# Linear attention: rotary pairs 64 partitions apart, halves exchanged by ScalarE, sine product and sum on GpSimd

## Chip, cores and metric

The kernel runs on one core of a Trainium2 chip. The metric is the device time of one execution in microseconds (us). TensorE is called PE, VectorE DVE, ScalarE ACT, GpSimd POOL and SyncE SP, as in the profile. SP issues all DMA transfers that this text speaks of.

## The reference

Sixteen sequences of 512 tokens with 128 features go through two layers. The stage that is changed here is the first one, causal linear attention with 16 heads of 8 features. Queries and keys are rotated by position, mapped by elu + 1, and the output at each token is a sum over all earlier tokens:

```
x = x + y                                  # y: depthwise convolution of 3 taps, then w_pw
qkv = einsum('btd,ed->bte', x, w_qkv)
q, k = _apply_rope(q, sin, cos), _apply_rope(k, sin, cos)
    # r1 = x1*cos - x2*sin ; r2 = x1*sin + x2*cos, pairs of neighbouring features
q_phi, k_phi = elu(q) + 1, elu(k) + 1
num   = q_phi . cumsum(k_phi * v)          # per head
denom = sum(q_phi * cumsum(k_phi))
attn  = num / (denom + 1e-6)
x = x + sigmoid(delta @ w_gate + b_gate) * (attn @ w_o)   # delta: x minus the token before
```

After it come a mixture of four experts, a routed layer, softmax attention and a second routed layer. They are left as they are.

## The kernel before

The stage is `attention_front`. It works on one sequence at a time, with features on the partitions and the 512 tokens along the free dimension. It is a software pipeline, written out by hand: each engine has a function `steps(b, u, n, f, c_)` that runs its share of one step, and `stages` calls it 19 times (the middle twelve in a loop of six rounds of two). In step s the engines work on four sequences at once: n = s is normalised, convolved and projected; f = s - 1 gets its rotary embedding and its feature map (q and k phi); b = s - 2 gets scores, state and weighted sum; c_ = s - 3 is divided, gated and normalised again. In a step with all four parts each engine goes through its list in the order written, and stops at the first wait that is not met. What other engines do does not change that order.

The names that matter here:

- `X` holds the input. SP loads sequence n with one transfer of 256 KB (L303). `stats(n)` on DVE (L700 and L703) is the first thing of a step on DVE and waits for that transfer; all of DVE's step stands behind it.
- `project` (L402) multiplies by the weights of q (n = 0) and k (n = 1) on PE. Each has two products, one with plain weights into bank 1 or 3 of PSUM (L409) and one with the weights of the exchanged pairs into bank 2 or 4 (L410).
- `rotate` (L706) on DVE multiplies bank 1 or 3 by the cosine and bank 2 or 4 by the signed sine, into `rot`. `rotated` (L714) adds the two and 1. `exps` (L614) on ACT makes the exponential `ex`, `phi` (L720) on DVE takes min(ex, 1) and the maximum with rot, into `qphi` or `kphi`.
- `stack` (L305) on SP copies qphi and kphi within SBUF into `qr` and `kr`, so that each head's 8 features lie on 8 neighbouring partitions at 0, 32, 64 or 96. It issues 4 transfers of 64 KB for q and 4 for k, each with 32 partitions as source and 8 as destination. `COPIES` is what their semaphores count to in a step.
- `scores` (L427) on PE multiplies kr by qr, 16 small products for each of 4 tiles t into banks 1 to 4. For t = 0 it waits until the projections of the next sequence have been read out of these banks (`qk_read`), and for the copies. `mask_scores` (L744) on DVE masks three of the banks into `am`, `raw_scores` (L618) on ACT copies the fourth, and `mask_last` (L341) on POOL masks it.
- `update_state` (L448) on PE and `mask_state` (L734) on DVE carry the sum over earlier tokens.
- `divide` (L756) on DVE is the division for c_; it waits for `copy_rdT` (L638) on ACT, and that for `turn_spread` (L487) on PE at the end of a step. `gate_tanh` (L643) is the gate on ACT.

In SP's list a step is: load X of n, then the copies for f. The load for step s therefore stands behind the copies that are issued in step s - 1.

Of the kernel before, what the change touches and what calls it, by code (L numbers as in the profile page):

```python
# [56 lines left out]
def _columns():  # L57
    at = 0
    for name, n in [("pw", P), ("q", P), ("qs", P), ("k", P), ("ks", P), ("v", P), ("o", P), ("gate", P),
                    ("moe_gate", MOE), ("dw", 3), ("b_gate", 1), ("ln_g", 1), ("ln_b", 1),  # L60
                    ("b1", MOE * MOE_CHUNKS), ("b2", MOE), ("router0", EXPERTS),
                    ("q1", P), ("k1", P), ("v1", P), ("router1", EXPERTS), ("br1", EXPERTS),
                    ("gamma", P), ("beta", P)]:
        WCOLS[name] = (at, at + n)
        at += n
    return at
# [122 lines left out]
def attention_front(nc, sems, X, w, c, PS, before, ones, minus_half, eps, scratch, H, LG, x):  # L189
# [4 lines left out]
    with ExitStack() as ctx:  # L194
# [52 lines left out]
        delta_ready = sem("delta_ready")  # L247
        qk_psum = sem("qk_psum"); qk_read = sem("qk_read"); rot_step = sem("rot_step"); exp_ready = sem("exp_ready")
        phi_ready = sem("phi_ready"); v_psum = sem("v_psum"); v_ready = sem("v_ready")
# [15 lines left out]

        COPIES = 16 * 4

# [29 lines left out]
        @block.sync  # L297
        def _(sp):
            def load(b):

                after_previous(sp, x_in, b, 16)
                src = x[bass.ds(b, 1), :, :].rearrange("o (c p) d -> p (o c) d", p=P)
                sp.dma_start(X[:, bass.ds(b * CT, CT), :], src).then_inc(x_in, 16)  # L303

            def stack(b, u):  # L305


                for which, (src, dst, signal) in enumerate([(qphi, qr, q_stacked), (kphi, kr, k_stacked)]):
                    sp.wait_ge(phi_ready, 2 * b + which + 1)
                    for j in range(4):  # L310
                        sp.dma_start(dst[32 * j:32 * j + HD, u, :, :], src[32 * j:32 * j + 32, u, :]).then_inc(signal, 16)

            def steps(b, u, n, f, c_):
                if n is not None:
                    load(n)
                if f is not None:
                    stack(f, 1 - u)
            stages(sp, steps)
            sp.wait_ge(x_in, 16 * BATCHES)

        @block.gpsimd
        def _(pool):
# [31 lines left out]
            def differences(f, u, c_):  # L354
                pool.wait_ge(x1_ready, f + 1)
                if c_ is not None:
                    pool.wait_ge(gate_psum, c_ + 1)
                nc.gpsimd.tensor_tensor(delta[:, 1 - u, 1:], x1T[:, 1 - u, 1:], x1T[:, 1 - u, 0:SEQ - 1],
                                        ALU.subtract).then_inc(delta_ready, 1)

            def weigh_keys(f, u):
                pool.wait_ge(kp_ready, f + 1)
                after_previous(pool, den_psum, f)
                nc.gpsimd.tensor_tensor(prod[:, :], qphi[:, 1 - u, :], kp[:, :], ALU.mult).then_inc(prod_ready, 1)

            def steps(b, u, n, f, c_):
                if n is not None:
                    inverse_deviation(n, ln1_stats, mv, ve, ve1_done, rstd, rstd1_ready, shift, shift1_ready, xn_ready, negated)
                if f is not None:
                    differences(f, u, c_)  # L370
                if b is not None:
                    mask_last(b, 0)
                    keep_x1(b, u)
                    mask_last(b, 1)
# [11 lines left out]
        def _(pe):  # L386
# [15 lines left out]
            def project(b, u, name, n):  # L402
                pe.wait_ge(x1_ready, b + 1)
                after_previous(pe, qk_read, b, 2)
                if since(b, 2):
                    pe.wait_ge(am_ready, 12 * (b + (-1)) - (1 - n))
                    if n:
                        pe.wait_ge(raw_ready, 4 * (b + (-1)))
                nc.tensor.matmul(PS[:, 1 + 2 * n, :], w(name), x1T[:, u, :], start=True, stop=True)  # L409
                nc.tensor.matmul(PS[:, 2 + 2 * n, :], w(name + "s"), x1T[:, u, :],  # L410
                                 start=True, stop=True).then_inc(qk_psum, 1)

# [155 lines left out]
        def _(act):  # L568
# [45 lines left out]
            def exps(b, n):  # L614
                act.wait_ge(rot_step, 6 * b + 3 * n + 3)
                nc.scalar.activation(ex[:, n, :], rot[:, n, 0, :], ACT.Exp, bias=minus_one[:, 0:1]).then_inc(exp_ready, 1)

# [39 lines left out]

            def steps(b, u, n, f, c_):
                if b is not None:
                    copy_k(b)  # L660
                if c_ is not None:
                    gate_tanh(c_)
                if f is not None:
                    exps(f, 0)
                    exps(f, 1)
                if b is not None:
# [5 lines left out]
                if b is not None:  # L672
                    raw_scores(b, 1)
                if n is not None:
                    copy_xnT(n)
# [17 lines left out]
        def _(dve):  # L693
# [12 lines left out]
            def rotate(b, n):  # L706


                after_previous(dve, phi_ready, b, 2)
                dve.wait_ge(qk_psum, 2 * b + n + 1)  # L710
                nc.vector.tensor_tensor(rot[:, n, 0, :], PS[:, 1 + 2 * n, :], c("cos"), ALU.mult).then_inc(rot_step, 1)
                nc.vector.tensor_tensor(rot[:, n, 1, :], PS[:, 2 + 2 * n, :], c("sin"), ALU.mult).then_inc(qk_read, 1)

            def rotated(b, n):  # L714
                dve.wait_ge(rot_step, 6 * b + 3 * n + 1)
                dve.wait_ge(qk_read, 2 * b + n + 1)
                nc.vector.scalar_tensor_tensor(rot[:, n, 0, :], rot[:, n, 0, :], 1.0, rot[:, n, 1, :],
                                               ALU.add, ALU.add).then_inc(rot_step, 2)

            def phi(b, u, n, dst):  # L720
                dve.wait_ge(exp_ready, 2 * b + n + 1)
                after_previous(dve, (q_stacked, k_stacked)[n], b, COPIES)
                nc.vector.scalar_tensor_tensor(dst[:, u, :], ex[:, n, :], 1.0, rot[:, n, 0, :], ALU.min,
                                               ALU.max).then_inc(phi_ready, 1)

# [64 lines left out]
            def steps(b, u, n, f, c_):  # L790
# [6 lines left out]
                if f is not None:  # L797
                    rotated(f, 0)
                    rotate(f, 1)
                    rotated(f, 1)  # L800
                    phi(f, 1 - u, 0, qphi)
                if b is not None:
                    mask_scores(b, 0)
                    mask_state(b, 0)
                if f is not None:
                    phi(f, 1 - u, 1, kphi)
                if c_ is not None:
                    close(c_)
                if b is not None:
                    invert(b)  # L810
                    mask_scores(b, 1)
                    mask_state(b, 1)
                if c_ is not None:
                    stats2(c_)
# [1264 lines left out]
def _stacked_rows():  # L2079

    p = np.arange(P)
    return 32 * (p % 4) + HD * (p // 32) + p % 32 // 4

# [26 lines left out]
def _layout(i):  # L2110
# [4 lines left out]
    t = {  # L2115
        "pw": i["L0_attn_w_pw"].T, "q": qkv[:P][nat].T, "qs": qkv[:P][nat ^ 1].T, "k": qkv[P:2 * P][nat].T,
        "ks": qkv[P:2 * P][nat ^ 1].T, "v": qkv[2 * P:].T, "o": i["L0_attn_w_o"].T, "gate": i["L0_attn_w_gate"].T,
        "moe_gate": i["L0_attn_w_moe_gate"].T, "dw": i["L0_attn_w_dw"], "b_gate": col(i["L0_attn_b_gate"]),
# [35 lines left out]
```

## Time and profile before

| | us |
|---|---|
| median of 3 runs | 1526.29 |
| range of the 3 runs | 1525.73 to 1536.03 |
| profiled execution, its own time | 1526.64 |
| profiled execution, span | 1524.8 |
| busy: PE / DVE / ACT / POOL | 1296.3 / 1003.6 / 801.9 / 689.2 |

The span is the time from the first to the last instruction in the profile; 1.8 us of the execution's own time lie around it. The stage in question covers roughly the first 472 us of the span, so the busy figures of the whole say little about it. The rows below are read from the trace by stretch and by instruction. In a timeline row the first number is the start in us from the start of the span, the second the time from the start of the first to the end of the last instruction of the row; "x3" is how many there are, and the brackets say how long the engine had been idle before and what released it. SPq rows are DMA issues. In a row for a stretch, DMA share is the mean busy share of the 16 DMA engines, and PEclk 1.00 stands for 2.4 GHz and 0.50 for 1.2 GHz.

### The profile page before, as it was taken

What the parts mean: (1) busy time and instruction counts of PE and PEld (TensorE: products, weight loads), DVE (VectorE), ACT (ScalarE), POOL (GpSimd) and SP (SyncE); (2) the same over time, 40 slices, a digit from 0 to 9 for tenths busy, and PEclk for the clock granted to TensorE, in tenths of its full rate; (3) what the DMA queues carried; (4) which work ended last, traced back from release to release, by engine and by line L of the source; (5) the groups of instructions that cost most, each with busy time, mean ns of one, the idle gap of its engine ahead of it and who ended that gap; (6) DMA issues with size and microseconds to landing.
All of it is one profiled execution on the core that took longest, in us unless ns stands there. A gap on an engine that the chain in (4) does not pass through costs nothing. (4 is left out here: it accounts for less than half of the span.)

```text
span 1524.8 us, 34022 instructions
## 1 busy us (share of the span) xinstructions
PE 1296.3 (85%) x10546; PEld 1013.7 (66%) x10546; DVE 1003.6 (66%) x3454; ACT 801.9 (53%) x1647; POOL 689.2 (45%) x845
## 2 busy tenths in 40 slices
PE   3899999999983999999999992667399999749996
PEld 1566666666652888888888881556277776539996
DVE  3677878787844788888888884456467777512221
ACT  2344444444423766666666660455266666525553
POOL 2344444444420044353444535223557788426665
PEclk9999999999975999999999996899699999969998
DMA  2231313131103000000000001556401112169881
GB/s 76 35 42 23 41 21 41 21 41 21 28 2 83 1 8 16 7 14 7 7 14 7 14 8 43 148 168 179 137 25 56 56 58 61 43 230 314 261 259 35
DMA packets 61579, 101.02 MB, mean 66 GB/s; under 512 B 9698, under 2 KB 36331, under 8 KB 61120
## 3 DMA queue, kind: packets, MB, share of 16 engines
q1 hardware_dynamic: 51648, 78.58, 20.1%
q0 software_dynamic: 9856, 21.52, 4.6%
q8 instruction: 37, 0.61, 0.2%
q14 instruction: 38, 0.31, 0.1%
HBM read 62.96 MB, written 29.75 MB: 61 GB/s over the span
## 5 line engine op out<-in xcount | busy, mean ns | idle before, releaser
L1138 DVE TENSOR_TENSOR m_Sl<-m_S,m_Sh 128x512 fp32r<-128x512 f32 x256 | 175.0, 693 | 32.5 <-ACT m_S L1050 27.6
L1050 ACT ACTIVATE m_S<-PS,W 128x512 f32<-128x512 f32 x256 | 175.3, 685 | 33.6 <-PE PS L958 30.5
L1413 POOL DMA_INDIRECT rows<-r_row,r_posi x128 | 139.7, 1091 | 37.4 <-issue 37.3
L1399 POOL TENSOR_TENSOR r_soft<-r_euler,r_soft 128x32 f32<-128x32 f32 x16 | 86.8, 5427 | 133.0 <-DVE r_soft L1295 133.0
L1045 ACT ACTIVATE m_Sh<-PS,W 128x512 fp32r<-128x512 f32 x128 | 88.1, 689 | 105.9 <-PE PS L958 105.6
L751 DVE TENSOR_TENSOR am<-PS,C 128x512 f32<-128x512 f32 x192 | 119.4, 676 | 20.5 <-PE PS L443 20.5
L956 PE MATMUL PS<-m_HH,m_w1h 128*128 128x512 f32 x256 | 110.8, 433 | 14.2 <-DVE m_HL L1102 14.0
L1631 PEld LDWEIGHTS PS<-f_wt,f_hid 128*128 128x128 f32 x960 | 119.6, 192 | 4.0
L1631 PE MATMUL PS<-f_wt,f_hid 128*128 128x128 f32 x960 | 120.0, 276 | 0.0
L1620 PE MATMUL PS<-f_xT,f_wt 128*128 128x256 f32 x480 | 119.6, 387 | 0.0
L344 POOL TENSOR_TENSOR am<-am,C 128x512 f32<-128x512 f32 x64 | 81.3, 1271 | 78.1 <-ACT am L624 78.1
L968 PE MATMUL PS<-m_Sh,m_w2h 128*128 128x512 f32 x256 | 102.0, 398 | 0.0
L958 PE MATMUL PS<-m_HH,m_w1l 128*128 128x512 f32 x256 | 101.8, 398 | 0.0
L957 PE MATMUL PS<-m_HL,m_w1h 128*128 128x512 f32 x256 | 101.7, 397 | 0.0
L971 PE MATMUL PS<-m_Sl,m_w2h 128*128 128x512 f32 x256 | 101.0, 395 | 0.0
L969 PE MATMUL PS<-m_Sh,m_w2l 128*128 128x512 f32 x256 | 100.6, 393 | 0.0
L1612 PE MATMUL PS<-C,f_row 128*128 128x128 f32 x160 | 34.0, 296 | 72.0 <-DMA f_row<-rows 72.0
L1709 DVE TENSOR_TENSOR f_res<-PS,f_xb 128x256 f32<-128x256 f32 x40 | 17.0, 425 | 118.8 <-PE PS L1631 118.8
L1620 PEld LDWEIGHTS PS<-f_xT,f_wt 128*128 128x128 f32 x480 | 87.2, 195 | 8.7
L1663 ACT ACTIVATE f_hid<-PS,f_wt 128x256 f32<-128x256 f32 x160 | 62.7, 474 | 55.0 <-PE PS L1620 54.8
L1593 POOL DMA_INDIRECT out<-f_res,f_token x80 | 79.2, 990 | 26.2 <-issue 26.2
L471 PE MATMUL PS<-am,vm 128*32 128x128 f32 x2048 | 80.3, 285 | 8.5 <-DVE am L751 7.1
(245 smaller groups left out, 3222.1 us busy)
## 6 DMA issues: line engine op xcount, KB each, us to landing
f_wt<-wr SPq DMA_DIRECT2D x40, 578.0 KB, 4.6
f_row<-rows SPq DMA_DIRECT2D x40, 260.0 KB, 2.9
f_wt<-wr SPq DMA_DIRECT2D x40, 256.0 KB, 2.9
f_row<-rows SPq DMA_DIRECT2D x40, 132.0 KB, 2.1
mid<-f_res SPq DMA_DIRECT2D x40, 128.0 KB, 2.7
rows<-r_padding SPq DMA_DIRECT2D x16, 260.0 KB, 3.3
X<-x SPq DMA_DIRECT2D x16, 256.0 KB, 5.4
qr<-qphi SPq DMA_DIRECT2D x64, 64.0 KB
```

What stands on the lines that cost most here:

```text
L751: nc.vector.tensor_tensor(am[:, j, :].rearrange("p (g q) -> p g q", g=4), PS[:, 1 + j, :].rearrange("p (g q) -> p g q", g=4), c("tri").uns ...
L956: nc.tensor.matmul(bank, w1h[:, f], HH[:, v, :], start=True, stop=False)
L957: nc.tensor.matmul(bank, w1h[:, f], HL[:, v, :], start=False, stop=False)
L958: nc.tensor.matmul(bank, w1l[:, f], HH[:, v, :], start=False, stop=True).then_inc(h_psum, 1)
L968: nc.tensor.matmul(bank, w2h[:, f], Sh[:, n % 4, :], start=(k == 0), stop=False)
L969: nc.tensor.matmul(bank, w2l[:, f], Sh[:, n % 4, :], start=False, stop=False)
L971: last = nc.tensor.matmul(bank, w2h[:, f], Sl[:, n % 4, :], start=False, stop=(k == MOE_CHUNKS - 1))
L1050: nc.scalar.activation(S[:, n % 3, :], PS[:, n % 3, :], ACT.Silu, bias=w("b1")[:, n:n + 1]).then_inc(s_ready, 1)
L1138: nc.vector.tensor_tensor(Sl[:, n % 4, :], S[:, n % 3, :], Sh[:, n % 4, :].bitcast(F32), ALU.subtract).then_inc(sl_ready, 1)
L1413: nc.gpsimd.indirect_dma_start(out=self.rows, out_offset=bass.IndirectOffsetOnAxis(ap=self.posi[:, u, t:t + 1], axis=0), in_=self.row[:, u ...
L1620: mm = nc.tensor.matmul(PS[:, 2 + 2 * (u % 2) + bank, half * SLOT:(half + 1) * SLOT], wt[:, u, f * P:(f + 1) * P], xT[:, u % 2, :], start= ...
L1631: mm = nc.tensor.matmul(PS[:, 6 + v, a * P:(a + 1) * P], hid[:, v, f, a * P:(a + 1) * P], wt[:, u, (chunks + f) * P:(chunks + f + 1) * P], ...
```

## The change

The features are laid out in another order over the partitions, so that the two features of a rotary pair lie 64 partitions apart. The projections with exchanged weights are gone. ACT copies partitions 64 to 127 of the projection to 0 to 63 and 0 to 63 to 64 to 127 (`swap_halves`), POOL multiplies this copy by the sine and adds it to DVE's product with the cosine (`sum_rotated`). elu + 1 is now min(exp, 1) + relu, with the relu on ACT. k needs one bank of PSUM instead of two, and its phi moves on DVE to a later place. With the new order of features one head's 8 features come from two halves, so each copy into qr or kr is split in two, of 16 partitions to 4.

```diff
-        COPIES = 16 * 4
+        COPIES = 16 * 8
                     for j in range(4):
-                        sp.dma_start(dst[32 * j:32 * j + HD, u, :, :], src[32 * j:32 * j + 32, u, :]).then_inc(signal, 16)
+                        for o in range(2):
+                            to = 32 * j + HD // 2 * o
+                            sp.dma_start(dst[to:to + HD // 2, u, :, :],
+                                         src[64 * o + 16 * j:64 * o + 16 * j + 16, u, :]).then_inc(signal, 16)
...
+            def sum_rotated(f, n):
+                pool.wait_ge(qk_read, 2 * f + n + 1)
+                nc.gpsimd.tensor_tensor(rot[:, n, 1, :], rot[:, n, 1, :], c("sin"), ALU.mult).then_inc(sin_done, 1)
+                pool.wait_ge(sin_done, 2 * f + n + 1)
+                nc.gpsimd.tensor_tensor(rot[:, n, 0, :], rot[:, n, 0, :], rot[:, n, 1, :], ALU.add).then_inc(rot_summed, 1)
...
                 if f is not None:
+                    sum_rotated(f, 0)
                     differences(f, u, c_)
                 if b is not None:
                     mask_last(b, 0)
+                if f is not None:
+                    sum_rotated(f, 1)
+                if b is not None:
                     keep_x1(b, u)
...
-                    pe.wait_ge(am_ready, 12 * (b + (-1)) - (1 - n))
-                    if n:
-                        pe.wait_ge(raw_ready, 4 * (b + (-1)))
-                nc.tensor.matmul(PS[:, 1 + 2 * n, :], w(name), x1T[:, u, :], start=True, stop=True)
-                nc.tensor.matmul(PS[:, 2 + 2 * n, :], w(name + "s"), x1T[:, u, :],
-                                 start=True, stop=True).then_inc(qk_psum, 1)
+                    pe.wait_ge(am_ready, 12 * (b + (-1)) - (2 - n))
+                nc.tensor.matmul(PS[:, 1 + n, :], w(name), x1T[:, u, :], start=True, stop=True).then_inc(qk_psum, 1)
...
             def exps(b, n):
-                act.wait_ge(rot_step, 6 * b + 3 * n + 3)
-                nc.scalar.activation(ex[:, n, :], rot[:, n, 0, :], ACT.Exp, bias=minus_one[:, 0:1]).then_inc(exp_ready, 1)
+                act.wait_ge(rot_summed, 2 * b + n + 1)
+                nc.scalar.activation(ex[:, n, :], rot[:, n, 0, :], ACT.Exp)
+                nc.scalar.activation(rot[:, n, 1, :], rot[:, n, 0, :], ACT.Relu).then_inc(exp_ready, 1)
+
+            def swap_halves(b, n):
+                act.wait_ge(cos_done, 2 * b + n + 1)
+                for o in range(2):
+                    ins = nc.scalar.activation(rot[64 - 64 * o:128 - 64 * o, n, 1, :], PS[64 * o:64 * o + 64, 1 + n, :], ACT.Copy)
+                ins.then_inc(qk_read, 1)
...
             def steps(b, u, n, f, c_):
+                if f is not None:
+                    swap_halves(f, 0)
                 if b is not None:
                     copy_k(b)
                 if c_ is not None:
                     gate_tanh(c_)
                 if f is not None:
+                    swap_halves(f, 1)
                     exps(f, 0)
-                    exps(f, 1)
...
                     raw_scores(b, 1)
+                if f is not None:
+                    exps(f, 1)
...
-                nc.vector.tensor_tensor(rot[:, n, 0, :], PS[:, 1 + 2 * n, :], c("cos"), ALU.mult).then_inc(rot_step, 1)
-                nc.vector.tensor_tensor(rot[:, n, 1, :], PS[:, 2 + 2 * n, :], c("sin"), ALU.mult).then_inc(qk_read, 1)
-
-            def rotated(b, n):
-                dve.wait_ge(rot_step, 6 * b + 3 * n + 1)
-                dve.wait_ge(qk_read, 2 * b + n + 1)
-                nc.vector.scalar_tensor_tensor(rot[:, n, 0, :], rot[:, n, 0, :], 1.0, rot[:, n, 1, :],
-                                               ALU.add, ALU.add).then_inc(rot_step, 2)
+                nc.vector.tensor_tensor(rot[:, n, 0, :], PS[:, 1 + n, :], c("cos"), ALU.mult).then_inc(cos_done, 1)
...
-                nc.vector.scalar_tensor_tensor(dst[:, u, :], ex[:, n, :], 1.0, rot[:, n, 0, :], ALU.min,
-                                               ALU.max).then_inc(phi_ready, 1)
+                nc.vector.scalar_tensor_tensor(dst[:, u, :], ex[:, n, :], 1.0, rot[:, n, 1, :], ALU.min,
+                                               ALU.add).then_inc(phi_ready, 1)
...
                 if f is not None:
-                    rotated(f, 0)
                     rotate(f, 1)
-                    rotated(f, 1)
-                    phi(f, 1 - u, 0, qphi)
                 if b is not None:
                     mask_scores(b, 0)
                     mask_state(b, 0)
                 if f is not None:
-                    phi(f, 1 - u, 1, kphi)
+                    phi(f, 1 - u, 0, qphi)
                 if c_ is not None:
                     close(c_)
                 if b is not None:
                     invert(b)
                     mask_scores(b, 1)
                     mask_state(b, 1)
+                if f is not None:
+                    phi(f, 1 - u, 1, kphi)
```

SP's list changes in the copies. One step of it in the program before, ahead of the loop (a row is line, operation, destination, source, shape of the destination, count; X is the input, qr and kr the stacked copies):

```order
L303 DMA X<-x 128x4x128
L311 DMA qr<-qphi 8x4x512 x4
L311 DMA kr<-kphi 8x4x512 x4
L303 DMA X<-x 128x4x128
L311 DMA qr<-qphi 8x4x512 x4
```

And the same place now:

```order
L303 DMA X<-x 128x4x128
L313 DMA qr<-qphi 4x4x512 x8
L313 DMA kr<-kphi 4x4x512 x8
L303 DMA X<-x 128x4x128
L313 DMA qr<-qphi 4x4x512 x8
```

Between two loads of X there are now 16 transfers instead of 8, each to 4 partitions instead of 8.

DVE's list for one step with all four parts, from the statistics' aggregation on, before (L711 and L712 are the products with cosine and sine, L717 the sum, L723 phi, L751 the masks of the scores, L736 that of the state, L759 the division):

```order
L711 TENSOR_TENSOR rot<-PS,C 128x512
L712 TENSOR_TENSOR rot<-PS,C 128x512
L759 TENSOR_TENSOR attn<-PS,spread 128x512
L717 SCALAR_TENSOR_TENSOR rot<-rot 128x512
L711 TENSOR_TENSOR rot<-PS,C 128x512
L712 TENSOR_TENSOR rot<-PS,C 128x512
L717 SCALAR_TENSOR_TENSOR rot<-rot 128x512
L723 SCALAR_TENSOR_TENSOR qphi<-ex,rot 128x512
L751 TENSOR_TENSOR am<-PS,C 128x512 x3
L736 TENSOR_TENSOR state<-PS,C 128x128
L723 SCALAR_TENSOR_TENSOR kphi<-ex,rot 128x512
```

And now (L731 is the product with the cosine, L736 phi, L749 the state's mask, L764 the masks of the scores, L772 the division, L777 and L780 `close`, L753 and L755 `invert`):

```order
L731 TENSOR_TENSOR rot<-PS,C 128x512
L772 TENSOR_TENSOR attn<-PS,spread 128x512
L731 TENSOR_TENSOR rot<-PS,C 128x512
L764 TENSOR_TENSOR am<-PS,C 128x512 x3
L749 TENSOR_TENSOR state<-PS,C 128x128
L736 SCALAR_TENSOR_TENSOR qphi<-ex,rot 128x512
L777 SCALAR_TENSOR_TENSOR x2T<-th,PS 128x512
L780 TENSOR_TENSOR x2T<-x2T,x1c 128x512
L753 TENSOR_SCALAR den<-PS 128x64
L755 RECIPROCAL den<-den 128x64
L764 TENSOR_TENSOR am<-PS,C 128x512 x3
L749 TENSOR_TENSOR state<-PS,C 128x128
```

The row that follows is phi of k. Two products and both sums are gone from DVE, phi of q stands behind the first masks, and phi of k behind the second ones.

## Rows read from the trace of the kernel before

**Rows 1.** Stretches, six rounds: length, busy time per engine, clock, DMA share, GB/s.

```profile
core 0: us, PE busy (x) PEld busy (x) DVE busy (x) ACT busy (x) POOL busy (x), PEclk, DMA share, GB/s
200.00:354.00 154.00, 143.67 (x1976) 100.05 (x1974) 121.60 (x290) 76.10 (x169) 66.76 (x96) 1.00 0.24 31
```

**Rows 2.** Timeline of DVE, statistics that open a step: start, us, what, idle before.

```profile
43.44 0.88 DVE L700 BATCH_NORM_STATS2 st<-X 128x6 f32<-128x128 f32 x4 [9.65 <-DMA X<-x]
...
65.81 0.86 DVE L700 BATCH_NORM_STATS2 st<-X 128x6 f32<-128x128 f32 x4
...
270.26 0.86 DVE L700 BATCH_NORM_STATS2 st<-X 128x6 f32 x4
...
372.92 0.86 DVE L700 BATCH_NORM_STATS2 st<-X 128x6 f32 x4
```

**Rows 3.** Timeline of one round, all engines: start, us, what, idle before.

```profile
251.34 0.68 DVE L712 TENSOR_TENSOR rot<-PS,C 128x512 f32<-128x512 f32 x1
...
252.27 1.17 PE L443 MATMUL PS<-qr,kr 8*128 8x128 f32 x32 [0.49 <-DVE rot L712]
...
253.37 0.68 DVE L723 SCALAR_TENSOR_TENSOR qphi<-ex,rot 128x512 f32<-128x512 f32 x1
...
255.76 0.27 DVE L736 TENSOR_TENSOR state<-PS,C 128x128 f32<-128x128 f32 x1
...
255.96 0.67 DVE L723 SCALAR_TENSOR_TENSOR kphi<-ex,rot 128x512 f32<-128x512 f32 x1
...
257.04 2.82 SPq L311 DMA_DIRECT2D kr<-kphi  x4
...
259.49 1.82 DVE L751 TENSOR_TENSOR am<-PS,C 128x512 f32<-128x512 f32 x3
...
260.18 0.39 SPq L303 DMA_DIRECT2D X<-x  x1
...
265.92 0.60 ACT L593 ACTIVATE x1T<-PS 128x512 f32<-128x512 f32 x1 [2.07 <-PE PS L399]
...
267.72 1.27 POOL L364 TENSOR_TENSOR prod<-qphi,kp 128x512 f32<-128x512 f32 x1 [1.91 <-DVE kp L731]
...
269.80 1.12 PE L409 MATMUL PS<-x1T,W 128*128 128x512 f32 x2 [0.78 <-DVE am L751]
...
271.82 0.69 DVE L711 TENSOR_TENSOR rot<-PS,C 128x512 f32<-128x512 f32 x1 [0.28 <-PE PS L410]
...
275.23 0.69 DVE L759 TENSOR_TENSOR attn<-PS,spread 128x512 f32<-128x512 f32 x1 [2.12 <-ACT spread L640]
```

**Rows 4.** Lines L303 and L311: issue time in ns, min/median/max; landing of X.

```profile
L303 SPq DMA_DIRECT2D X<-x x16: 385/398/443, 8.8 to 362.8; - x16
...
DMA to landing us min/median/max: 2.8/5.4/5.8
...
L311 SPq DMA_DIRECT2D kr<-kphi x64: 659/672/1184, 34.8 to 413.5; - x64
```

**Rows 5.** Stretches while only the copies of qphi and kphi move (columns as rows 1).

```profile
257.00:261.00 4.00, 3.75 (x64) 3.09 (x56) 3.13 (x7) 2.07 (x6) 1.98 (x3) 1.00 0.56 63
...
258.40:259.40 1.00, 1.00 (x11) 1.00 (x11) 0.61 (x2) 0.23 (x2) 1.00 (x2) 1.00 0.52 51
```

**Rows 6.** Stretches around the idle time of PE in step 1 (columns as rows 1).

```profile
30.00:33.00 3.00, 0.00 (x0) 0.00 (x0) 2.64 (x5) 1.92 (x5) 0.00 (x0) 1.00 0.00 0
33.00:36.00 3.00, 1.08 (x4) 0.71 (x4) 0.79 (x1) 1.73 (x7) 1.26 (x1) 0.57 0.39 84
...
39.00:42.00 3.00, 2.31 (x5) 0.85 (x4) 0.00 (x0) 0.60 (x1) 0.00 (x0) 0.79 0.91 88
```

**Rows 7.** Timeline of step 1: first DVE product, qphi, PE after its idle time.

```profile
26.90 0.69 DVE L711 TENSOR_TENSOR rot<-PS,C 128x512 f32<-128x512 f32 x1 [9.61 <-PE PS L410]
...
30.97 0.68 DVE L723 SCALAR_TENSOR_TENSOR qphi<-ex,rot 128x512 f32<-128x512 f32 x1
...
34.62 1.08 PE L393 MATMUL PS<-C,xn 128*128 128x128 f32 x4 [5.14 <-ACT vm L611]
```

More of the change, by code:

```diff
@@ L58, in _columns @@
     at = 0
-    for name, n in [("pw", P), ("q", P), ("qs", P), ("k", P), ("ks", P), ("v", P), ("o", P), ("gate", P),
+    for name, n in [("pw", P), ("q", P), ("k", P), ("v", P), ("o", P), ("gate", P),
                     ("moe_gate", MOE), ("dw", 3), ("b_gate", 1), ("ln_g", 1), ("ln_b", 1),
@@ L247, in attention_front @@
         delta_ready = sem("delta_ready")
-        qk_psum = sem("qk_psum"); qk_read = sem("qk_read"); rot_step = sem("rot_step"); exp_ready = sem("exp_ready")
+        qk_psum = sem("qk_psum"); qk_read = sem("qk_read"); rot_summed = sem("rot_summed"); cos_done = sem("cos_done"); sin_done = sem("sin_done"); exp_ready = sem("exp_ready")
         phi_ready = sem("phi_ready"); v_psum = sem("v_psum"); v_ready = sem("v_ready")
@@ L2081, in _stacked_rows @@
     p = np.arange(P)
-    return 32 * (p % 4) + HD * (p // 32) + p % 32 // 4
+    return 32 * (p % 4) + HD * (p % 64 // 16) + 2 * (p % 16 // 4) + p // 64
 def _constants():
@@ L2115, in _layout @@
     t = {
-        "pw": i["L0_attn_w_pw"].T, "q": qkv[:P][nat].T, "qs": qkv[:P][nat ^ 1].T, "k": qkv[P:2 * P][nat].T,
-        "ks": qkv[P:2 * P][nat ^ 1].T, "v": qkv[2 * P:].T, "o": i["L0_attn_w_o"].T, "gate": i["L0_attn_w_gate"].T,
+        "pw": i["L0_attn_w_pw"].T, "q": qkv[:P][nat].T, "k": qkv[P:2 * P][nat].T, "v": qkv[2 * P:].T, "o": i["L0_attn_w_o"].T, "gate": i["L0_attn_w_gate"].T,
         "moe_gate": i["L0_attn_w_moe_gate"].T, "dw": i["L0_attn_w_dw"], "b_gate": col(i["L0_attn_b_gate"]),
```

## Prediction

> **What bounds the kernel now.** I first read the stretch of six rounds (a round is one pass through the step with all four parts) in the middle of the stage: of 154.0 us PE is busy 143.67, DVE 121.60, ACT 76.10, POOL 66.76 [rows 1]. So PE is nearly full, with DVE close behind. A round lasts (372.92 - 65.81) / 12 = 25.6 us, from the statistics that open step 3 to those that open step 15 [rows 2]. Taking work off PE and DVE could therefore pay, as long as nothing else becomes late. ACT and POOL have room.
>
> Next I read one round in order of time [rows 3], and asked of each wait what ends it last. PE waits for DVE's last read of the projections before it starts the scores (0.49 us), and for a DVE mask before the projection of q (0.78 us). DVE waits 2.12 us for the division's input at the turn of a step. The chain runs PE, ACT, DVE and back, with small waits everywhere.
>
> Third, SP. It shows no wait of an engine inside the loop, but it has a chain of its own: phi of q ends on DVE at 253.37 + 0.68 = 254.05, four copies of q, phi of k ends at 256.63, four copies of k from 257.04 on, and only then, at 260.18, the load of X [rows 3]. With a median of 5.4 us to its landing [rows 4] X is there at 265.6. The statistics need it at 270.26 [rows 2]. The slack is 4.7 us. Only in step 2 did DVE wait for X, 9.65 us [rows 2].
>
> **The change, what it takes away.** PE loses two products per round. One product takes 1.12 us from start to end [rows 3], less behind another one; I take 0.9, so 1.8 us of PE's 23.9 busy (143.67 / 6). The wait for the mask goes down by one mask, 0.6 us. DVE loses two products and two sums of 0.6 to 0.7 us, some 2.6 us.
>
> **What it adds on the chain.** Between DVE's product with the cosine and the scores now stand two ACT copies of 64 partitions. The nearest row is a copy of 128 x 512 out of PSUM, 0.60 us [rows 3]; one issued behind the other ends 0.5 later, so 1.1 us for a pair. Were time to go with partitions it would be 0.6; I keep 1.1, since nothing in the rows makes a narrower copy faster. POOL gets four operations of 1.27 us [rows 3] per round, 5.1 us, on an engine busy 11.1 of 25.6. ACT gets 2.2 us of copies and two relus of about 0.6. For q, POOL's pair, exp and relu take about 4 us behind the exchange and lie beside the scores and the state update; without that cover they would cost up to 2.
>
> **What it does to SP's chain.** There are two effects. First, phi of k moves behind the second masks: these end at 261.31, the state mask at about 261.5, phi at 262.2 instead of 256.63, 5.5 us later [rows 3]. Second, 16 transfers stand ahead of X instead of 8. SP's issue of one takes 0.67 us at 64 KB, while that of X takes 0.40 at 256 KB [rows 4], so bytes do not set it; 8 copies of k take 8 x 0.71 = 5.7 us to issue (2.82 / 4 each [rows 3]), half if it went with size.
>
> The service is dearer. While only these copies move, 9 of the 16 DMA engines are busy (0.56) and 63 GB/s flow [rows 5]: one transfer of 65.5 KB per 1.04 us. X, 4 times as large and spread over 128 partitions, lands in 2.8 us at best [rows 4]. So a transfer to 8 partitions is limited by where it goes. The new one goes to 4 partitions, each of which still gets 8 KB. I take the same 1.04 us for it, as if half the lanes did the same work each; the bound below is 0.52, half the bytes at the same rate, and the bound above 1.28, from the slowest stretch of 1 us, at 51 GB/s [rows 5].
>
> The Trainium skill ("DMA: Bandwidth & Descriptors", section "Why a DMA increments its semaphore by 16 and not by 1") says that a transfer runs on the largest number of engines up to 16 that divides the outermost dimension of both sides: 8 for 8 and 32 partitions, 4 for 4 and 16. The busy share agrees for the former; no row here shows the latter. The skill ("SBUF — State Buffer", section "Door 1: The DMA port swizzle") also has 4 neighbouring partitions share one port of 27.2 GB/s, an estimate of 54 GB/s for 8 partitions against the 63 measured, and 1.2 us for one new transfer. By it the sum would be 16 x 0.16 x 14 = 36 us more, 1655.
>
> **The new round.** Start with X landed, S.
> - Statistics until S + 1.3 (270.26 to where DVE began to wait, 271.82 - 0.28 [rows 2, 3]), then three DVE operations 0.61 apart: cosine of q, division, cosine of k, to S + 3.2.
> - ACT: q's exchange from S + 2.0 to 3.1, its copy of k and the tanh (0.6 each, as the copy's row) to 4.3, k's exchange to 5.4. Scores start at S + 5.5.
> - From the start of the scores to the state's mask it is 255.76 - 252.27 = 3.5 us [rows 3]; with mask (0.27) and phi (0.68), phi of q ends at S + 9.9.
> - From there to the landing of X it was 265.6 - 254.05 = 11.5 us with 8 transfers. Eight more at 1.04 make 19.8. The later phi of k hides in this: it ends about 6 us after phi of q, when q's eight are still being served (8.3 us).
>
> That closes a ring of 9.9 + 19.8 = 29.7 us, longer than 25.6: DVE waits for X in every step, and all that PE and DVE saved is idle time.
>
> **The clock.** PE then works 23.9 - 1.8 = 22.1 of 29.7 us, and most of the 7.6 idle is one piece ahead of the scores. In step 1 PE stood idle 5.14 us until 34.62 [rows 7]; the granted clock fell to 0.50 and stayed there until about 40.3 [rows 6], 5.6 us after work came back, at 1.2 instead of 2.4 GHz. That cost 2.8 us of work. The new round has 3.3 us of PE work between the start of the scores and the state update, on the ring. I charge 2.2 us, between 0 and 2.8 and near the row, since part may meet waits for DVE. The round is 31.9.
>
> **The sum.** Step 2: first cosine at 26.90 [rows 7], 0.9 earlier with one pair fewer; 0.7 product, 1.1 exchange, 2.6 POOL, 1.2 exp and relu, 0.7 phi, gaps 0.1 each: phi of q ends at 32.5 instead of 31.65 [rows 7]. With 43.44 - 31.65 = 11.8 and 8.3 more, statistics start at 52.6, +9.2. Step 2 to 3, without division, tanh and output projection: 19.8 + 7.6 + 2.2 = 29.6 against 22.37, +7.2. Twelve rounds at 31.9 - 25.6 = 6.3: +75.7. Behind step 15 no X is loaded; there I take nothing (PE gains 2, the clock takes it back). Together +92, on the profiled execution's own time of 1526.64, which is within 0.4 us of the median: 1619.
>
> **Rivals.**
> - *The clock holds.* PE's idle time falls into pieces. Then 13 x 2.2 = 29 us less: 1590. For it: the clock is 1.00 through all six rounds [rows 1], but there no idle piece is long. Chance 0.22.
> - *Copies served as fast as they are issued* (0.52 us each, below the 0.71 of the issue). Then only phi of k and the issue count: 262.2 + 0.4 + 5.7 + 0.3 = 268.6, landing 271.4 to 274.0, 1.1 to 3.7 late, of which the 2.12 us of DVE's idle time [rows 3] absorb most: 0 to 1.6 per round. The exchange takes back on the way to the scores what PE's products gave. With 4 to 6 us in step 2: 1531 to 1554, say 1543. For it: X's own rate. Chance 0.25, nearly half of it within 1%.
> - *Faster.* PE's relief decides. X would have to land within 8 us of the new phi of k (270.26 - 262.2), and the exchange stay hidden; then a round is 1.8 us shorter, 12 rounds 22 us: 1505. Against it: X landed 9.0 us after phi of k with half the transfers. Chance 0.05.
>
> **Numbers.** Main case 0.45, the clock holding 0.22, fast copies 0.25, faster 0.05, and 0.03 for worse than all. Range 1540 to 1655: from the middle of the fast-copy case up to two thirds of what transfers of 1.28 us would add (16 x 0.24 x 14 = 54 us); about 0.15 lies below and 0.05 above. A change under 1% can't be told from none. Faster by over 1% 0.05, within 1% 0.12, slower 0.83. The likeliest case's own range is 1600 to 1655.
>
> **What would show it.** In the profile after: statistics on DVE released by the DMA of X in 14 steps, for 5 us or more; a round of 32 us; a busy share near 0.27 while the copies move, with 30 GB/s; low clock in each round. If DVE waits for X only in step 2, the ring is wrong. If it waits and the share stays at 0.56, the service price is. If rounds last 29.7 with the clock at 1.00, only the clock is.

## The result and the profile after

The change makes the kernel slower: 1558.12 us (median of 4 runs, 1556.75 to 1558.82) against 1527.01 us, a ratio of 1.0203 with a 95% interval of 1.0181 to 1.0224. That is 31 us, where the prediction had 92. (A fourth run has moved the median of the kernel before from 1526.29 to 1527.01.) The profiled execution has a span of 1556.3 us, 31.5 more than before.

The page of the changed kernel gives the busy time of each engine, share of the span and instructions:

```profile
PE 1302.2 (84%) x10482; PEld 1022.8 (66%) x10482; DVE 970.5 (62%) x3390; ACT 853.4 (55%) x1743; POOL 775.1 (50%) x909
```

DVE works 33 us less than before, ACT 52 and POOL 86 us more. PE is at 1302.2 against 1296.3, although it has 64 matmul records fewer.

Where the time went is read as in [rows 2], from the statistics that open each step on DVE (start, duration, idle time before and its releaser):

```profile
47.73 0.87 DVE L720 BATCH_NORM_STATS2 st<-X 128x6 f32<-128x128 f32 x4 [9.50 <-DMA X<-x]
...
75.51 0.67 DVE L720 BATCH_NORM_STATS2 st<-X 128x6 f32<-128x128 f32 x3
```

```profile
266.12 0.87 DVE L720 BATCH_NORM_STATS2 st<-X 128x6 f32 x4 [1.12 <-DMA X<-x]
...
293.19 0.87 DVE L720 BATCH_NORM_STATS2 st<-X 128x6 f32 x4 [0.92 <-DMA X<-x]
```

```profile
402.38 0.87 DVE L720 BATCH_NORM_STATS2 st<-X 128x6 f32 x4 [1.04 <-DMA X<-x]
```

Step 2 opens at 47.73 instead of 43.44 (+4.3), step 3 at 75.51 instead of 65.81 (5.4 more), and the twelve rounds from step 3 to step 15 take 326.87 instead of 307.11, 27.24 us each instead of 25.59 (19.8 more). That makes 29.5 of the 31.5 us. The rest is scattered behind step 15. DVE waits for X in 13 steps (14 were forecast), but for 1 us in a round and not for 5 or more.

One round in order of time, all engines, to be read against [rows 3]:

```profile
268.87 0.69 DVE L772 TENSOR_TENSOR attn<-PS,spread 128x512 f32<-128x512 f32 x1 [0.88 <-ACT spread L656]
...
271.17 1.19 ACT L631 ACTIVATE rot<-PS 64x512 f32<-64x512 f32 x2
...
272.60 1.17 PE L452 MATMUL PS<-qr,kr 8*128 8x128 f32 x32 [2.35 <-ACT rot L631]
...
273.71 1.37 PE L512 MATMUL PS<-attn,W 128*128 128x512 f32 x2
273.76 1.89 DVE L764 TENSOR_TENSOR am<-PS,C 128x512 f32<-128x512 f32 x3 [3.61 <-PE PS L452]
...
274.87 1.91 PE L424 MATMUL PS<-W,x1T 128*128 128x128 f32 x8
...
277.14 1.14 PEld L480 LDWEIGHTS PS<-am,vm 128*32 128x32 f32 x32 [0.23 <-issue]
...
277.46 1.55 DVE L736 SCALAR_TENSOR_TENSOR qphi<-ex,rot 128x512 f32<-128x512 f32 x1
278.48 0.98 PEld L452 LDWEIGHTS PS<-qr,kr 8*128 8x128 f32 x32 [0.20 <-issue]
...
283.35 0.68 DVE L736 SCALAR_TENSOR_TENSOR kphi<-ex,rot 128x512 f32<-128x512 f32 x1
```

```profile
284.63 5.31 SPq L313 DMA_DIRECT2D kr<-kphi  x8
290.27 0.39 SPq L303 DMA_DIRECT2D X<-x  x1
```

The order of events is the one of the prediction. The exchange of k (L631, two copies, 1.19 us) ends at 272.36 and lets the scores start at 272.60, for which PE had waited 2.35 us; before it was 0.49 [rows 3]. The copies of k take 5.31 us to issue, and X is issued at 290.27, 2.9 us ahead of the statistics that need it. But X lands in 2.8 us, not in 5.4 and not behind a queue. Behind X there is a second wait that the prediction did not have: DVE stands 0.88 us in front of the division (L772), until ACT has copied its input out of PSUM (L656). Lines L303 and L313, issue time in ns and landing in us, as in [rows 4]:

```profile
L303 SPq DMA_DIRECT2D X<-x x16: 385/394/441, 8.4 to 399.3; - x16
...
  DVE st L720: 22.1, 13
...
DMA to landing us min/median/max: 2.5/2.8/2.9
```

```profile
L313 SPq DMA_DIRECT2D kr<-kphi x128: 613/626/820, 39.5 to 452.2; - x128
```

The copies in the changed kernel, in the columns of [rows 5] (length, busy time of each engine, clock, DMA share, GB/s):

```profile
285.50:289.50 4.00, 4.00 (x50) 2.48 (x52) 3.54 (x6) 1.93 (x6) 2.70 (x5) 1.00 0.15 48
```

Only 0.15 of the DMA engines' time is in use, and 48 GB/s is about what the issue allows (one transfer of 32.8 KB per 0.66 us would be 49). Before, the copies kept 0.56 of the engines' time busy at 63 GB/s [rows 5].

The clock does fall, once in each round. Two neighbouring stretches of one round:

```profile
216.00:219.50 3.50, 1.44 (x33) 1.31 (x34) 0.28 (x1) 3.04 (x7) 3.10 (x3) 1.00 0.00 0
219.50:223.50 4.00, 4.00 (x32) 3.04 (x34) 2.33 (x5) 3.18 (x10) 3.36 (x3) 0.57 0.00 0
```

In the first PE is busy 1.44 of 3.5 us: the idle time in front of the scores, which are waiting for the exchange. In the second it is busy throughout, and 0.57 is the mean of 2.4 GHz and 1.2 GHz with most of the stretch at the lower. So the four products of v (L424; a product leaves two records) take 1.91 us in the round above, and the state's update ends late.

### The profile page after: what moved, and what is told of

Read it like the earlier page. It is cut to its first block and busy times, and to the rows that moved or that the text cites. A ratio compares the mean times of both kernels' runs of the same rounds, so it can differ in the third digit from the quotient of the medians.

```text
span 1556.3 us, 34066 instructions
## 1 busy us (share of the span) xinstructions
PE 1302.2 (84%) x10482; PEld 1022.8 (66%) x10482; DVE 970.5 (62%) x3390; ACT 853.4 (55%) x1743; POOL 775.1 (50%) x909
## 3 DMA queue, kind: packets, MB, share of 16 engines
q1 hardware_dynamic: 51648, 78.45, 16.3%
## 5 line engine op out<-in xcount | busy, mean ns | idle before, releaser
L764 DVE TENSOR_TENSOR am<-PS,C 128x512 f32<-128x512 f32 x192 | 119.5, 678 | 74.3 <-PE PS L452 74.3
L968 PE MATMUL PS<-m_HH,m_w1h 128*128 128x512 f32 x256 | 110.7, 433 | 14.2 <-DVE m_HL L1114 14.1
L452 PE MATMUL PS<-qr,kr 8*128 8x128 f32 x2048 | 78.1, 291 | 39.6 <-ACT rot L631 39.6
L452 PEld LDWEIGHTS PS<-qr,kr 8*128 8x128 f32 x2048 | 65.9, 193 | 62.0 <-issue 48.7
L480 PE MATMUL PS<-am,vm 128*32 128x128 f32 x2048 | 85.5, 300 | 8.5 <-DVE am L764 7.1
```

Source lines behind the costliest of these rows:

```text
L452: mm = nc.tensor.matmul(PS[:, 1 + j, g * P:(g + 1) * P], kr[rows, u, g, cols], qr[rows, u, g, cols], start=True, stop=True)
L764: nc.vector.tensor_tensor(am[:, j, :].rearrange("p (g q) -> p g q", g=4), PS[:, 1 + j, :].rearrange("p (g q) -> p g q", g=4), c("tri").uns ...
L968: nc.tensor.matmul(bank, w1h[:, f], HH[:, v, :], start=True, stop=False)
```

## The experiments

**The split copies alone, in the kernel before.**

```diff
-        COPIES = 16 * 4
+        COPIES = 16 * 8
-                        sp.dma_start(dst[32 * j:32 * j + HD, u, :, :], src[32 * j:32 * j + 32, u, :]).then_inc(signal, 16)
+                        for o in range(2):
+                            to = 32 * j + HD // 2 * o
+                            sp.dma_start(dst[to:to + HD // 2, u, :, :],
+                                         src[32 * j + 16 * o:32 * j + 16 * o + 16, u, :]).then_inc(signal, 16)
```

> The kernel before with one part of the change alone: each copy of 32 partitions to 8 is split in two of 16 to 4, still 8 + 8 transfers, everything else as before. Theory A (a transfer to 4 partitions is served as fast as it is issued, because neighbouring transfers go to different places): k's copies end their issue 2.5 us + 2.5 us later, X is issued near 265 and lands near 268, ahead of the statistics at 270.3; rounds stay at 25.6 us, only step 2 is late by some 2 us: 1527 to 1530. Theory B (the price of the prediction, 1.04 us each): X lands 8.3 us later than 265.6, 3.6 us behind the need, of which 2.1 are absorbed: rounds of 27 us and more, 1545 or above.

Measured: 1529.71 us, ratio 1.0009 (0.9992 to 1.0026), no difference that this measurement can tell. A round in the middle of the stage and its copies (statistics on DVE, then a stretch with only copies, then the landing of X):

```profile
278.44 0.86 DVE L703 BATCH_NORM_STATS2 st<-X 128x6 f32 x4
...
304.14 0.86 DVE L703 BATCH_NORM_STATS2 st<-X 128x6 f32 x4
```

```profile
192.00:196.00 4.00, 3.83 (x60) 2.37 (x61) 3.96 (x15) 0.60 (x1) 1.82 (x5) 1.00 0.15 49
```

```profile
DMA to landing us min/median/max: 2.7/2.8/3.0
```

The round is 25.70, without a wait for X. The share is 0.15 and X lands in 2.8 us, as in the changed kernel. So the doubled number of transfers is no part of the loss in the rounds, and the prediction's price for them is refuted with this one part alone.

One early round of this profiled execution is longer, 28.91 us, and it is the clock:

```profile
95.55:124.46 28.91, 27.22 (x330) 18.75 (x329) 20.26 (x49) 12.69 (x29) 11.13 (x16) 0.88 0.10 30
```

The run with the unsplit copies in another order (the last one below) has the same round, 28.92 us at 0.88, so it doesn't come from the split. PE's longest idle piece in it and right ahead of it is 0.87 us.

**Two filler products on PE in front of the first scores, in the changed kernel.**

```diff
+                if b is not None and f is not None:
+                    after_previous(pe, am_ready, b, 12)
+                    for _ in range(2):
+                        nc.tensor.matmul(PS[:, 3, :], w("q"), c("cos"), start=True, stop=True)
                 if b is not None:
                     scores(b, u, 0, f)
```

> The changed kernel with two products of 512 columns added on PE between the gate and the first scores, into a bank of PSUM that is free then; their results are never read. PE stands idle 2.35 us there. Theory A (what makes the round 1.6 us longer is the low clock behind this idle time): the clock stays at 1.00 in the rounds and a round returns to about 25.7 us: 1535 to 1540. Theory C (the exchange on the way to the scores and the late X set the round): the fillers change nothing or cost up to 0.5 us a round: 1556 to 1565.

Measured: 1539.47 us, ratio 1.0063 (1.0036 to 1.009), 18.7 us less than the changed kernel. One round, PE (L541 are the two fillers, with two records each, L452 the scores, L424 the products of v):

```profile
286.10 1.88 PE L541 MATMUL PS<-C,W 128*128 128x512 f32 x4
288.62 1.17 PE L452 MATMUL PS<-qr,kr 8*128 8x128 f32 x32 [0.64 <-ACT rot L635]
...
290.69 1.05 PE L424 MATMUL PS<-W,x1T 128*128 128x128 f32 x8
```

```profile
200.00:364.00 164.00, 154.24 (x2076) 104.62 (x2069) 114.66 (x278) 99.14 (x212) 103.10 (x126) 0.99 0.10 31
```

```profile
200.00:364.00 164.00, 144.80 (x1956) 102.59 (x1958) 109.79 (x266) 95.93 (x206) 97.44 (x121) 0.94 0.09 29
```

The last row is the same stretch of the changed kernel, the one above it that of this run. With more work on PE the clock is at 0.99 instead of 0.94, the products of v take 1.05 us instead of 1.91, and a round takes 26.1 on average, (387.08 - 73.70) / 12. Useless work makes the kernel faster; the scores start no earlier for it, and what differs is the clock behind them.

In two of the twelve rounds the clock still falls, later in the round and with PE at work. One of them, cut at its statistics, and three us inside it:

```profile
176.91:203.34 26.43, 25.11 (x324) 16.34 (x323) 18.31 (x44) 15.18 (x33) 16.21 (x20) 0.94 0.09 30
195.00:198.00 3.00, 3.00 (x5) 1.10 (x4) 2.08 (x4) 0.24 (x1) 2.59 (x4) 0.51 0.14 45
```

PE's longest idle piece in this round is 0.64 us. So work in the idle piece takes the fall out of ten rounds of twelve, but a fall doesn't need a piece of that length. What it does need is open.

**X loaded one sequence further ahead, in the changed kernel.** SP's loop is written out, with three loads ahead of the first copies and the load of f + 3 behind the copies of f.

```diff
-            stages(sp, steps)
+            for n in range(3):
+                load(n)
+            for f in range(BATCHES):
+                stack(f, f % 2)
+                if f + 3 < BATCHES:
+                    load(f + 3)
```

> The changed kernel with X loaded one sequence further ahead, so that no load stands behind the copies of the step before its use. Theory A: DVE's waits of 1.0 us for X in the rounds lie in front of a longer wait for the division's input and cost nothing there; only the 9.5 us in step 2 count, some 5 to 8 us: 1550 to 1554. Theory C (X sets the round): another 1.0 us in each of 12 rounds, 1538 to 1542.

Measured: 1552.36 us, ratio 1.0154 (1.012 to 1.0188), 5.8 us less than the changed kernel. Statistics of two steps:

```profile
340.58 0.86 DVE L725 BATCH_NORM_STATS2 st<-X 128x6 f32 x4
...
367.84 0.86 DVE L725 BATCH_NORM_STATS2 st<-X 128x6 f32 x4
```

```profile
290.05 0.69 DVE L777 TENSOR_TENSOR attn<-PS,spread 128x512 f32<-128x512 f32 x1 [2.17 <-ACT spread L661]
```

The wait for X is gone, and the round is 27.26, as long as in the changed kernel. There it stands in front of the wait for the division's input, which was 0.88 us and is 2.17 now: the 1 us of the one is taken off the other. All of the gain is in the first steps.

**The eight copies in another order, in the changed kernel.**

```diff
-                    for j in range(4):
-                        for o in range(2):
+                    for o in range(2):
+                        for j in range(4):
```

> The changed kernel with the same 8 transfers per tensor in another order: first the four of one half, then the four of the other, so that transfers to partitions 0-3 and 32-35, and 64-67 and 96-99, follow each other. Theory A (the slow service of the kernel before comes from successive transfers to the same group of partitions 32 apart; alternating between 0-3 and 4-7 hides it): a transfer takes 0.9 to 1.2 us again, X lands 4 to 5 us later, DVE waits for it some 5 us in each round, rounds of 29 to 31 us: 1585 to 1610. Rival B2 (only the smaller size made them fast): nothing changes, 1556 to 1560.

Measured: 1558.74 us, ratio 1.0199 (1.0158 to 1.0241). A stretch with only copies, and the landing of X:

```profile
258.00:262.00 4.00, 4.00 (x73) 2.81 (x71) 2.71 (x5) 2.00 (x5) 2.64 (x4) 1.00 0.20 53
```

```profile
DMA to landing us min/median/max: 2.8/3.2/4.2
```

The share goes from 0.15 to 0.20 and X lands 0.4 us later. Neighbours in the same group do cost something, but nowhere near the price that this theory named; the expected 1585 to 1610 was a miss. Whether the order or the size makes most of the price can't be told from this run.

**The exchange of k ahead of the gate's tanh, in the changed kernel.**

```diff
                 if b is not None:
                     copy_k(b)
+                if f is not None:
+                    swap_halves(f, 1)
                 if c_ is not None:
                     gate_tanh(c_)
                 if f is not None:
-                    swap_halves(f, 1)
                     exps(f, 0)
```

> The changed kernel with one order on ACT altered: the exchange of k's halves stands ahead of the gate's tanh, so that the scores start 0.7 us earlier. Theory A (the exchange's delay leaves PE idle 2.35 us, and this idle time is what lets the clock fall): a round is 0.7 us shorter even if the clock falls as before (12 rounds, about 9 us: 1547 to 1550), and up to 2.3 us shorter in rounds in which the shorter idle time no longer lets it fall (down to 1530). If X sets the round: no change, 1556 to 1560.

Measured: 1542.18 us, ratio 1.0095 (1.0062 to 1.0128), 16 us less than the changed kernel. PE's wait in front of the scores is 1.78 us instead of 2.35:

```profile
264.82 1.17 PE L452 MATMUL PS<-qr,kr 8*128 8x128 f32 x32 [1.78 <-ACT rot L631]
```

Taking 0.6 us off the wait gives 16 us and not the 7 of twelve times 0.6: the clock now falls in seven of the twelve rounds and not in all.

**Fillers and early X together.** The two edits shown above in one kernel.

> The changed kernel with both the two filler products on PE and the load of X one sequence earlier. If the two causes are separate, their gains add: 1558.1 - 18.7 - 5.8 = 1533.6, 1530 to 1537. If X is hidden by the low clock and comes out once the clock is held, the sum is larger than that: below 1530.

Measured: 1530.67 us, ratio 1.0021 (0.9998 to 1.0043). From step 4 on all rounds are 25.86 long with the clock at 1.00:

```profile
324.88 0.86 DVE L729 BATCH_NORM_STATS2 st<-X 128x6 f32 x4
...
350.73 0.86 DVE L729 BATCH_NORM_STATS2 st<-X 128x6 f32 x4
```

The gains add, and 3 us more than that (1533.6 was the sum). These 3 us are about two falls of the clock: the fillers alone had left two, and with X early, so that DVE's steps are evenly spaced, there is none.

**Exchange first and early X, without fillers.**

> The changed kernel with the exchange of k ahead of the tanh and X one sequence earlier, without fillers. From the run with the exchange alone (1542.2), less the 5.8 us that the early X gave: 1536 if the clock falls in as many rounds as there (8 of 12 low), 1520 to 1525 if the now regular rounds keep it up, as with the fillers.

Measured: 1535.21 us, ratio 1.0052 (1.0032 to 1.0071), the first of the two expected values. This run shows the price of the clock within one kernel. Four rounds, cut at the statistics that open them:

```profile
194.33:221.09 26.76, 24.14 (x326) 16.92 (x325) 18.14 (x45) 15.93 (x35) 16.13 (x20) 0.94 0.09 27
221.09:247.78 26.69, 24.08 (x326) 17.10 (x325) 17.61 (x45) 15.93 (x35) 16.48 (x20) 0.94 0.10 32
247.78:272.88 25.10, 22.49 (x326) 15.81 (x325) 17.61 (x45) 15.90 (x35) 16.89 (x20) 1.00 0.10 31
272.88:299.64 26.76, 24.15 (x326) 16.93 (x325) 18.13 (x45) 15.93 (x35) 16.16 (x20) 0.94 0.09 28
```

Every third round runs at full clock and takes 25.10 us; the others have a mean clock of 0.94 and take 26.7. PE has the same 326 matmul records in each and is busy 22.49 us in the one, 24.1 in the others. One fall costs 1.6 us here.

**All three together.**

> The changed kernel with the fillers, the earlier X and the exchange of k ahead of the tanh. Theory A: 0.5 to 0.7 us a round less than the kernel with the first two, 1524 to 1529; the fillers may then stand in front of the scores and give part of it back.

Measured: 1520.17 us, ratio 0.9951 (0.9928 to 0.9974). This is faster than both kernels, and better than the 1524 to 1529 that were expected. A round is 25.10 us:

```profile
268.73 0.86 DVE L730 BATCH_NORM_STATS2 st<-X 128x6 f32 x4
...
293.83 0.86 DVE L730 BATCH_NORM_STATS2 st<-X 128x6 f32 x4
```

**The same with one filler product instead of two.**

```diff
-                    for _ in range(2):
+                    for _ in range(1):
```

> The version that beats both kernels, with one filler product instead of two. If one is enough to hold the clock, as fast as with two or up to 0.3 us a round faster, since nothing stands in front of the scores: 1516 to 1520. If not, the clock falls in some rounds: 1525 to 1540.

Measured: 1519.44 us, ratio 0.9954 (0.9924 to 0.9984). One product of 512 columns per round is enough here; rounds are 25.10 too. Whether it works by filling part of the idle piece or by adding work, these runs don't tell apart.

**The kernel before with X one sequence earlier.**

> The kernel before with X loaded one sequence earlier. In its rounds X lands 4.7 us ahead of its need, so only the 9.65 us of DVE's wait in step 2 can go, of which the changed kernel got back 5.8 us: 1520 to 1523. If no gain: the wait in step 2 lies beside another one.

Measured: 1524.1 us, ratio 0.9987 (0.9968 to 1.0007), not told apart from before, and short of the 1520 to 1523 that were expected; its rounds are as long as they were. By the medians the early X is worth 2 us here, so it does not make up the 6 to 7 us of the best version. The rest is in the rounds, 25.10 against 25.6.

**The kernel before with its copies in the order j = 0, 2, 1, 3.**

```diff
-                    for j in range(4):
+                    for j in (0, 2, 1, 3):
```

> The kernel before with its four copies per tensor in the order j = 0, 2, 1, 3, so that no two neighbouring transfers go to partitions 32 apart (0-7 and 32-39). The prediction priced a transfer at 1.04 us from the row of 63 GB/s. If that price comes from neighbouring transfers that share their destination's group, it falls to the 0.7 us of the issue, the busy share of the DMA engines falls below 0.45 while the copies move, and X lands in about 3 us instead of 5.4. If it comes from the width of a transfer (64 KB from eight engines to eight partitions), all stays as it was: 0.56, 63 GB/s, 5.4 us. The time is 1526 either way.

Measured once: 1527.54 us. A stretch of the copies (X is issued in its last us), and the landing of X:

```profile
262.50:266.50 4.00, 3.75 (x61) 3.04 (x56) 3.14 (x7) 2.02 (x5) 1.97 (x3) 1.00 0.51 71
```

```profile
DMA to landing us min/median/max: 2.7/4.0/4.5
```

The landing of X goes from 5.4 to 4.0 us, about half of the way to the 2.8 of the narrower transfers; the busy share, from 0.56, hardly comes down towards 0.15. So the order of neighbours is a part of the price of a transfer, and the larger part is something in its shape that no run here takes apart.

## Why the prediction was wrong in size

**What bounds the kernel, and what the engines gain: right in the main.** At full clock PE is busy 22.49 us in a round (exchange first and early X) against 23.9, 1.4 less where 1.8 was forecast. DVE is busy 18.2 (109.79 us in 164) against 20.3, 2.0 less where 2.6 was forecast, with phi of q at 1.55 us instead of 0.68 in it. The exchange of halves takes 1.19 us a pair against the 1.1 of the working. X is issued 17.7 us behind the start of the scores, where the working of the fast copies had 268.6 - 252.27 = 16.3. Phi of k ends 11.4 us behind that start instead of 4.4, which is 7.1 later and not 5.5: the low clock and the longer phi of q lie in between.

**The service of the copies: the step that failed.** The term was "I take the same 1.04 us for it, as if half the lanes did the same work each". Measured, no backlog forms behind the transfers to 4 partitions (X lands in 2.8 us), so one takes no more than its issue, 0.66 us, with the DMA engines 0.15 busy against the 0.56 of before. The lower bound that the working had written down, 0.52, was the nearer one. The row of 63 GB/s was a rate under a backlog, and I read from it a cost per destination partition that no row showed. With 16 transfers per round this single term made the ring of 19.8 + 9.9 us. In the trace X lands 290.27 + 2.8 - 279.01 = 14.1 us after the end of phi of q, not 19.8. DVE still waits for it, about 1 us in a round, but the early X (rounds unchanged at 27.26) shows that this wait costs nothing, and the kernel before with split copies shows that the number of transfers doesn't lengthen its rounds either. The condition that the prediction set itself, a busy share near 0.27 and 30 GB/s, was not met either: 0.15 and 48.

**The other half of the ring.** From the landing of X to the end of phi of q the working had 9.9 us and 2.2 for the clock; it is 279.01 - 266.12 = 12.9. One us of it is lost before the scores, which start 6.5 us behind the statistics and not 5.5: the working set the division right behind the first cosine, and gave no time to the wait for its input. 12.9 + 14.1 = 27.0 is the measured round (266.12 to 293.19), so X does arrive just in time in each step, but without that wait the round is no shorter. What sets it is the path from PE's end of the step over ACT's copy to the division, the cosine of k, its exchange and the scores; with the clock held, 0.6 us less on this path makes a round 0.75 shorter (25.86 to 25.10).

**The clock: right in kind, and near in size.** It was charged 2.2 us per round, for an idle piece of more than 5 us made by the wait for X. The piece is 2.35 us long and made by the exchange, and even so the clock falls in each round. It costs 1.6 us by the rounds of one kernel with and without a fall, and 1.4 by the kernels with early X, without and with fillers (27.26 against 25.86). That is nearly all of what the rounds lose, 1.65. The cause was mistaken even so: the wait for X, which was to make the idle piece, makes none of it. With X early the piece is 2.35 us as before, and the clock falls as before.

**The balance behind it.** From the start of the division to the start of the scores it is 272.60 - 268.87 = 3.7 us, against 2.7 before (252.27 + 25.65 - 275.23 [rows 3]): the exchange costs 1.0 us there. With the clock held (fillers and early X) a round of the changed kernel is 25.86, against 25.6, and with the exchange 0.6 us earlier it is 25.10. So what PE gained by two products fewer is given back by the exchange, as the rival of the fast copies had it. That rival (1543, up to 1554) had the right mechanism for the transfers and nothing for the clock; 13 falls of 1.6 us, 21 us, on top of its 1531 to 1554 give 1552 to 1575, and the measured 1558 lies in that. This sum is made afterwards. Only the range as a whole, 1540 to 1655, held the result beforehand, and it held it by the width given to the rivals. The cases had been drawn up as if the low clock could only follow from a long wait for X.

**The first steps.** Step 2 was forecast 9.2 late and is 4.3 late; step 3 7.2 more and is 5.4 more. At the end of the 9.5 us that DVE waits there for X stands the issue of the transfers and not their service: k's copies are issued from 39.53 to 44.80, X at 44.84, and it has landed at 47.7.

**The two rules that were weighed.** That a transfer runs on the largest number of engines that divides both outer dimensions, the Trainium skill ("DMA: Bandwidth & Descriptors", section "Why a DMA increments its semaphore by 16 and not by 1"), would allow 4 of 16 engines here. The share of 0.15 lies below the 0.25 of four busy ones and does not contradict it. The port of 27.2 GB/s that the Trainium skill ("SBUF — State Buffer", section "Door 1: The DMA port swizzle") gives to 4 neighbouring partitions would make 1.2 us for a transfer, an estimate. No run here has transfers to one group alone: the 48 to 53 GB/s flow where transfers to several groups can be under way at once, which neither confirms nor refutes the figure. The order of the loops matters in the direction of that rule (0.15 against 0.20, and the faster landing of X in the kernel before).

## What to carry to other kernels

A step that adds a fixed delay in front of PE near its limit can cost twice where it opens an idle piece: once in the chain and once in the clock of PE. Look in the profile after for rounds with a mean clock below 1.00, and test with useless products in the idle piece; if the kernel gets faster, shorten the wait that opens it, or leave one product in. A transfer rate read from a backlog is no price for a transfer of another shape: without a row of that shape, both bounds have to carry weight.

## What the runs showed of the hardware that I had not expected

- The narrower transfers are far cheaper: 16 partitions to 4 in 32 KB needs 0.15 of the DMA engines' time at 48 to 49 GB/s, while 32 partitions to 8 in 64 KB needs 0.56 at 63 GB/s, almost three times as much per byte. Splitting each copy in two halved the landing time of the load behind them, 5.4 to 2.8 us. Their order changes part of it; what makes the rest is open.
- The clock fell from 2.4 to 1.2 GHz in every round although PE's longest idle piece was 2.35 us and PE was busy 144.80 of 164 us. With 1.78 us it fell in seven of twelve rounds. It did not fall in the rounds of the version with all three edits, with two products of 512 columns in that piece or with one. But it also fell where PE's longest idle piece in the round was 0.64 us (fillers alone) or 0.87 us (split copies in the kernel before, one round), so the length of a piece doesn't decide it alone.
- Phi of q on DVE takes 1.55 us instead of 0.68 where POOL's sum of k lies beside it, and phi of k, with nothing of POOL beside it, takes 0.68:

```profile
277.19 1.28 POOL L368 TENSOR_TENSOR rot<-rot 128x512 f32<-128x512 f32 x1
```

  In the version with all three edits it is the other way round: phi of q takes 0.69, and POOL's product of k beside it 1.72 instead of 1.26. What this costs a round no run takes apart.
